# Attention kernel: on SyncE's queue, the move of the fourth unit's maxima and sums put ahead of the next half's stack loads

## What is computed

```python
scores = jnp.einsum('bhqd,bhkd->bhqk', q, k) * scale
scores = scores * smask          # smask[i, j] = ((i & j) == 0)
a = jax.nn.softmax(scores, axis=-1)
att = jnp.einsum('bhqk,bhkd->bhqd', a, v)
```

## Time and profile before

| | |
|---|---|
| median of 3 runs | 2054.38 us (2048.66 to 2054.62) |
| the profiled execution's own time | 2054.39 us |
| its span | 2052.6 us |
| mean granted TensorE clock | 0.902 |
| TensorE busy | 1663.9 us (81%) |
| VectorE busy | 1405.7 us (68%) |
| ScalarE busy | 1180.1 us (57%) |
| GpSimd busy | 254.5 us (12%) |
| moved by DMA | 130.83 MB, mean 64 GB/s |

### The profile page before, as it was taken

The page is one execution under the profiler, slowest core; times in us unless marked ns, Lnnn a source line. Parts: engine busy times, 40 slices in busy tenths (PEclk is TensorE's granted clock), DMA queues, the critical chain, the costliest instruction groups (busy, mean ns, idle before and its releaser), DMA issues.

```text
span 2052.6 us, 66915 instructions
## 1 busy us (share of the span) xinstructions
PE 1663.9 (81%) x28905; PEld 919.2 (45%) x28905; DVE 1405.7 (68%) x3285; ACT 1180.1 (57%) x2117; POOL 254.5 (12%) x229
## 2 busy tenths in 40 slices
PE   2889999997453779897988889797979787979677
PEld 1123333332341355554555555554555554545445
DVE  7788888881674667675766758585767675757824
ACT  2057777776212366665766757575756566756542
POOL 1000000000003002120302112121202021202010
PEclk8589999999775799999998989899999999999889
DMA  6022102000005333325242423332333423242001
GB/s 149 15 48 75 37 2 48 3 3 1 13 0 131 89 91 77 86 55 132 50 113 50 125 62 89 64 103 60 91 71 85 100 71 82 57 130 50 6 2 31
DMA packets 152204, 130.83 MB, mean 64 GB/s; under 512 B 65013, under 2 KB 147381, under 8 KB 149893
## 3 DMA queue, kind: packets, MB, share of 16 engines
q1 hardware_dynamic: 151909, 126.55, 25.8%
HBM read 79.25 MB, written 45.88 MB: 61 GB/s over the span
## 4 chain that ended last, share of the span: by engine, by line
PE 45%; DVE 23%; ACT 11%; DMA 10%; issue 7%; SPq 4%; POOL 1%; ACTq 0%; POOLq 0%; DVEq 0%
PE pB L605 10%; PE pO L620 9%; PE pA L590 8%; DVE mx L847 6%; DMA sce<-emx 5%; ACT PB L718 5%; PE pG L561 4%; PE pG L571 4%; SPq L937 2%; PE pG L511 2%; DVE bst L427 2%; DVE N L443 1%; DMA QS<-scq 1%; ACT VD L678 1%; DVE x L732 1%
## 5 line engine op out<-in xcount | busy, mean ns | idle before, releaser
L718 ACT ACTIVATE PB<-pB 128x512 f32<-128x512 f32 (+1 forms) x1496 | 831.1, 594 | 367.3 <-PE pB L605 352.1
L847 DVE TENSOR_REDUCE mx<-pA 128x1 f32<-128x512 f32 (+3 forms) x1000 | 633.3, 669 | 121.7 <-PE pA L590 120.5
L605 PE MATMUL pB<-QS,KS 85*32 85x256 bf16 (+3 forms) x11264 | 598.2, 284 | 55.1 <-ACT PB L718 30.5
L590 PE MATMUL pA<-KS,QS 82*32 82x256 bf16 (+2 forms) x8384 | 545.6, 312 | 75.3 <-DMA QS<-scq 47.1
L620 PE MATMUL pO<-PB,VD 128*32 128x128 f32 (+3 forms) x5632 | 457.4, 397 | 8.2 <-issue 5.3
L605 PEld LDWEIGHTS pB<-QS,KS 85*32 85x32 bf16 x11264 | 260.8, 97 | 337.4 <-ACT PB L718 230.8
L590 PEld LDWEIGHTS pA<-KS,QS 82*32 82x32 bf16 x8384 | 204.9, 97 | 290.6 <-DVE mx L847 101.4
L450 POOL TENSOR_TENSOR rstd<-vareps,mhalf 128x4 f32<-128x4 f32 x68 | 69.2, 1018 | 1185.3 <-DVE vareps L436 1184.2
L847 DVE TENSOR_REDUCE mxb<-pA 128x1 f32<-128x512 f32 x304 | 206.7, 680 | 9.5 <-PE pA L590 8.1
L620 PEld LDWEIGHTS pO<-PB,VD 128*32 128x32 f32 x5632 | 159.6, 111 | 39.3 <-issue 10.0
L754 DVE TENSOR_TENSOR ON<-pG,em 128x288 f32<-128x288 f32 x48 | 21.9, 457 | 176.1 <-ACT em L663 138.6
(11 more groups left out here) (160 smaller groups left out, 1616.1 us busy)
## 6 DMA issues: line engine op xcount, KB each, us to landing
scq<-PQ SPq DMA_DIRECT2D x84, 384.0 KB, 3.6
QS<-scq SPq DMA_DIRECT2D x56, 576.0 KB
KS<-sck SPq DMA_DIRECT2D x84, 384.0 KB
sck<-PK SPq DMA_DIRECT2D x28, 384.0 KB, 5.3
wL<-in_wL SPq DMA_DIRECT2D x6, 576.0 KB, 4.9
emr<-sce SPq DMA_DIRECT2D x192, 4.0 KB, 1.8
QS<-mt SPq DMA_DIRECT2D x168, 8.0 KB, 2.2
rE<-in_rE SPq DMA_DIRECT2D x7, 256.0 KB, 12.0
```

What stands on the lines that cost most here:

```text
L590: ins = pe.matmul(pA[QT * hd:QT * (hd + 1), a.a_bank(half, n), at:at + width], QS[0:R_A, r // NR, head, r % NR * QT:(r % NR + 1) * QT], ro ...
L605: ins = pe.matmul(pB[32 * i:32 * (i + 1), a.b_bank(h, v), at:at + width], KS[0:R_B, head, k0:k0 + 32], allowed(QS[0:R_B, x, head, :], 3, k ...
L718: act.activation(PB[:, pos_, 0:st.cols], pB[:, a.b_bank(h, v), 0:st.cols], ACT.Exp).then_inc(a.b_exped, 1)
L847: v.tensor_reduce(dst[:, gs[0]:gs[-1] + 1, tl[0]:tl[-1] + 1:step], pA[:, a.a_bank(half, n), 0:len(gs) * len(tl) * st.width] .rearrange("p ...
```

## The change

The move of unit 3 of a sparse half is taken from the start of the next half's order, and put right behind the move of unit 2, ahead of `load_k(h+1, 0)` and `load_q(h+1; 0, 1)`. The dense halves keep their order. Nothing is computed differently.

```diff
         def sp_half(sp, a, half, between=None):
 
             cur, prev, nxt = a.alive(half), a.alive(half + -1), a.alive(half + 1)
-            if prev:
+            if prev and not a.sparse:
                 move_max(sp, a, half + -1, 3)
             if cur and a.sparse:
                 load_q(sp, a, half, 1, 0)
@@
                 load_q(sp, a, half + 1, 0, 0)
             if cur:
                 move_max(sp, a, half, 2)
+            if cur and a.sparse:
+                move_max(sp, a, half, 3)
             if nxt:
                 load_k(sp, a, half + 1, 0)
                 load_q(sp, a, half + 1, 0, 1)
```

## The result

The changed kernel took 2076.43 us (median of 4 runs, 2071.06 to 2083.43), the kernel before 2054.50 us (median of 4). The ratio is 1.0113, 95% interval 1.0076 to 1.0150: slower by about 22 us, 2.0 us at each of the eleven borders. It was forecast at 2058 us, within 2042 to 2076. The profiled execution took 2083.43 us, the slowest of the four, with a span of 2081.6 us; 4 us of that had been lost ahead of the encoder's first A step, where nothing is changed. So what follows reads stretches at the borders, not ends.

What follows compares the result with a forecast made beforehand. It took the eleven borders between encoder halves to hold the kernel up, `em3` waiting for the `emx` write behind the stack loads. Stack +2, clock +4 and VectorE -2.5 gave +3.5 us on 2054.4: 2058 us, range 2042 to 2076.

Steps and rivals of the forecast that it cites:

- The hole stays and changes its owner: At each border TensorE waits some 9.5 us for the stack, where it stood 9.10 us at line 525.
- The stack, +2 us: Next half's stack lands later, maxima ready plus 19.0 us, gating the first A step: about +2 us over eleven borders.
- The clock, +4 us: After the hole, TensorE restarts with slot 9, so more slots run at half speed: 0.4 us a border, +4 us.
- Work no longer behind the hole, -2.5 us: VectorE's last product of line 754 no longer stands between hole and first maxima: half of 0.46 us a border.
- Weights at nothing, the dense halves at nothing: Even halves' weight loads start about 7 us later, but some 37 us cover them: no cost.
- My own second sign of being wrong: The forecast is wrong if the slots after the gap from unit 3's maxima to the first A step change pace.
- My slower rival: SyncE is held longer by unit 3's move, over 5.8 us: 2072 to 2082 us, chance 0.33.

Runs made afterwards that it cites:

- e_only: Changed kernel with unit 3's three `mt` DMAs put back behind the stack loads, only the `emx` write and read-back ahead: 2049.6 us, ratio to before 0.9981.
- hole_vm3: Changed kernel with TensorE made to wait for the stack already ahead of `vm3`, nothing else moved: 2080.4 us, ratio to before 1.0121.
- warm_after: Changed kernel with 34 unused filling matmuls between `vm3` and slot 9's wait for the stack: 2062.6 us, ratio to before 1.0037.
- weave_warm: `weave` with 16 filling matmuls before slot 9's wait for the stack: 1989.7 us, ratio to before 0.9670.
- e_warm: `e_only` with 26 filling matmuls before slot 9's wait for the stack: 2033.5 us, ratio to before 0.9895.
- warm_before: Kernel before with the 34 filling matmuls in its own hole, ahead of `vm3`'s wait: 2049.7 us, ratio 0.9967.
- weave: All on SyncE, unit 3's `emx` write and read-backs placed between `load_k`'s three DMAs, `mt` last, against the kernel before: 2011.8 us, ratio 0.9806.
- act_q: Kernel before with unit 3's `emx` write and read-back issued by ScalarE instead of SyncE, `mt` behind the loads: 2036.2 us, ratio 0.9917.

## Why the prediction was wrong

*The hole stays and changes its owner*: right. ScalarE's wait fell by 91 us (forecast 107), TensorE's for the stack rose by 102 us, eleven times more (forecast about 100). `em3` came 7.9 us after the maxima, not 6.6: each landing of `emx` took 2.0 us (1.68 in the row I used), and from the first read-back to `em3` it was 3.8 us (3.14 there).

*The stack, +2 us*: right in kind, short in size. The move took 6.2 us from the maxima to `load_k`, not 5.8; from there to the first A step it was 13.1 us (I had 13.2). The gap went from 18.8 to 19.4 us: 0.5 us a border, 6 us in all, where I had 0.2. `e_only` shows that SyncE's time passes into it one for one. Part of the longer move is the landing, 2.04 us on average where I had taken the row's 1.68. The Trainium skill, page DMA: Bandwidth & Descriptors, under the table on where the 2 us go, has a fixed cost of about 2.0 us, which it fits to DMAs that GpSimd issues. SyncE's landed in 2.04 us, so the traces agree, and it was the better figure: it would have given 3.5 us more.

*The clock, +4 us*: **the step that failed.** I let the stretch at half clock after the first A step grow by at most 1.9 us, took 0.8, and priced it at 0.49 us each. It grew by 2.8 us. The price was right: the runs give 0.47 us for each, above 17.9 us with none. The run went from 19.1 to 20.6 us, 1.5 us a border and 16 us in all, where this term had 4. The argument I had taken at less than half, that TensorE restarts with slot 9 and not with `vm3` ahead of it, was true in full and even understated: `hole_vm3`, which moves nothing but the place of the hole, takes back the whole stretch, and `warm_after`, which fills the hole, takes back 3.2 us of it.

*Work no longer behind the hole, -2.5 us*: nothing of it was seen. The run grew by 1.5 us where 2.8 us more at half clock account for 1.3 to 1.4, which leaves no gain of VectorE's.

*Weights at nothing, the dense halves at nothing*: no cost is seen. The rest of a half took 71.0 us before and 71.4 and 70.1 after; under a microsecond these profiles can't tell.

My own second sign of being wrong, slots at another pace behind a gap of 19.4 us, is what came. My slower rival had the right sign and a nearly right price (2072), but that is luck: its mechanism, SyncE held longer, came to 0.4 us a border, some 5 of the 22 us, and 16 are the clock's, for which it had 5.5. The end of my range, 2076.0, was 0.4 us short of the median.

## What to carry to other kernels

When two gates stand close to each other, moving one ahead of the other on one queue moves the wait, and every microsecond of issue and landing that goes in front is paid in full; look for an order in which neither stands behind the other whole, as small transfers between pieces of a large one. After a hole in TensorE's work count what runs next at half clock, too: here it cost 0.47 us for each microsecond. A hole that moves takes that cost to other instructions, and work passed ahead of it is hardly won: of 1.7 us, 1.5 came back. Filling a hole paid where the filling was about as long as it (`weave_warm`), paid in part where 2 us were left open (`warm_after`, `e_warm`), and paid nothing where it was longer (`warm_before`).

## What the runs showed of the hardware that was not expected

A 16 KB write takes 8.4 to 8.9 us to land behind a 1.7 MB load of another engine's queue, against 9.8 us behind it on the same queue, 3.3 us with one third of `load_k` ahead of it (`weave`) and 2.0 us ahead of it. And a hole of 3.7 us on average (`weave`) cost as much half-clock time in the run, 5.8 us, as one of 9.3 us did (5.4 us, after). The length of a hole alone did not tell the cost; where it stood did: 2.6 us with `vm3` behind it, none in the run with 6.4 us of work behind it (`act_q`, at the border shown; the half clock then fell in the gap).
